# Expert stage of a two-layer kernel: the ids are turned ahead of the similarities on TensorE and ScalarE, and GpSimd gates the rows of `up` ahead of the slots' ids

## The reference, cut to what matters

```python
h = layernorm(x) * (1 + cb) + sb
q = batch_normalised(h @ w_q)                   # per token 2 sides x 8 heads x 128
sim = einsum('pbnhd,hkpd->pbnhk', q, keys)      # 32 keys on each side
sx, ix = top_k(sim[0], 8)
sy, iy = top_k(sim[1], 8)
scores, pk = top_k(sx[..., :, None] + sy[..., None, :], 8)   # 8 of 64 pairs
indices = (ix * 32 + iy) taken at pk            # ids of 8 experts per head
w = softmax(scores) * gelu(h . down_embed[indices])
x = x + gb * sum of w * up_embed[indices]
```

## Time and profile before

| | |
|---|---|
| runs of the kernel before, us | 3028.55 median of 3 (3027.59 to 3028.96) |
| the profiled execution, us | 3042.62, with a span of 3040.8 |
| busy, of the span | TensorE 91%, VectorE 75%, ScalarE 72%, GpSimd 58% |
| 29 units of the expert stage, from 1944.42 to 2759.18 us | 814.76 |
| of them busy | VectorE 771.62, TensorE 739.68, ScalarE 520.69, GpSimd 276.86 |
| mean granted TensorE clock there | 0.78 of full speed |

### The profile page before, as it was taken

The page is one execution under the profiler, slowest core; times in us unless marked ns, Lnnn a source line. Parts: engine busy times, 40 slices in busy tenths (PEclk is TensorE's granted clock), DMA queues, the critical chain, the costliest instruction groups (busy, mean ns, idle before and its releaser), DMA issues. The chain is left out here.

```text
span 3040.8 us, 77592 instructions
## 1 busy us (share of the span) xinstructions
PE 2775.4 (91%) x27940; PEld 2091.0 (69%) x27940; DVE 2294.6 (75%) x8471; ACT 2180.4 (72%) x4273; POOL 1777.8 (58%) x1756
## 2 busy tenths in 40 slices
PE   5999999999999999999999985799989899998688
PEld 3777777777777777777777774566666666666443
DVE  5676776767767767767767645899999999997565
ACT  3888888887888887887887860566666666665575
POOL 3788887788779878878778770333333333331111
PEclk7999999999999999999999996687777777777799
DMA  3000000000000000000000003000000000000000
GB/s 103 1 1 8 1 1 8 1 1 8 1 1 8 1 1 8 1 1 8 1 1 8 1 8 123 1 0 0 0 0 0 0 0 0 0 0 2 8 21 28
DMA packets 11793, 27.63 MB, mean 9 GB/s; under 512 B 1529, under 2 KB 6137, under 8 KB 11137
## 3 DMA queue, kind: packets, MB, share of 16 engines
q1 hardware_dynamic: 11618, 25.48, 2.5%
HBM read 17.07 MB, written 8.40 MB: 8 GB/s over the span
## 5 line engine op out<-in xcount | busy, mean ns | idle before, releaser
L284 POOL TENSOR_TENSOR probs_l<-probs,probs_h 128x512 fp32r<-128x512 f32 x1024 | 1302.3, 1294 | 342.7 <-ACT probs_h L378 339.0
L377 ACT ACTIVATE probs<-bank 128x512 f32<-128x512 f32 x1024 | 636.0, 621 | 280.3 <-PE bank L698 200.7
L539 DVE TENSOR_REDUCE maxes<-ring 128x1 f32<-128x512 f32 x1024 | 659.7, 686 | 185.0 <-PE ring L678 184.2
L378 ACT ACTIVATE probs_h<-bank 128x512 fp32r<-128x512 f32 x1024 | 636.9, 622 | 0.0
L697 PE MATMUL bank<-q_hh,k_hl 128*128 128x512 f32 x1024 | 425.7, 416 | 1.8 <-ACT probs_h L378 1.6
L698 PE MATMUL bank<-q_lm,k_h 65*128 65x512 f32 x1024 | 406.7, 397 | 0.0
L708 PE MATMUL obank<-probs_h,x_l 128*128 128x512 f32 x1024 | 405.5, 396 | 0.0
L710 PE MATMUL obank<-probs_h,x_h 128*128 128x512 f32 x1024 | 404.5, 395 | 0.0
L709 PE MATMUL obank<-probs_l,x_h 128*128 128x512 f32 x1024 | 403.8, 394 | 0.0
L678 PE MATMUL ring<-k_hl,q_hh 128*128 128x512 f32 x1024 | 339.3, 412 | 12.0 <-DVE maxes L539 7.4
L1074 ACT ACTIVATE low_hot<-obank 128x512 f16<-128x512 f32 x512 | 296.9, 603 | 66.0 <-PE obank L1249 52.9
(11 more groups left out here) (252 smaller groups left out, 4986.2 us busy)
## 6 DMA issues: line engine op xcount, KB each, us to landing
xt<-in_x SPq DMA_DIRECT2D x8, 512.0 KB, 9.5
out_x<-xt SPq DMA_DIRECT2D x8, 512.0 KB, 2.6
x<-out_x SPq DMA_DIRECT2D x1, 4096.0 KB, 12.1
out_x<-x SPq DMA_DIRECT2D x16, 256.0 KB, 2.1
mod<-out_x SPq DMA_DIRECT2D x3, 512.0 KB, 13.7
pk_wq<-in_w_q SPq DMA_DIRECT2D x1, 1024.0 KB, 5.9
pk_wqT<-in_w_qT SPq DMA_DIRECT2D x1, 1024.0 KB, 7.4
hot_rule<-in_hot_rule SPq DMA_DIRECT2D x1, 776.0 KB
```

Of the source, the lines that this page charges most:

```text
L284: nc.gpsimd.tensor_tensor(probs_l[:, i, :], probs[:, s % 4, :], probs_h[:, i, :].bitcast(F32), ALU.subtract).then_inc(low_ready, 1)
L377: nc.scalar.activation(probs[:, s % 4, :], st[s % 4], ACT.Exp)
L378: nc.scalar.activation(probs_h[:, i, :], st[s % 4], ACT.Exp).then_inc(st_free[s % 4], 1)
L539: nc.vector.tensor_reduce(maxes[:, i, k:k + 1], ring[bank_of(at)][:], AX.X, ALU.max).then_inc(rows_maxed, 1)
```

## The change

Three lists of calls are put in another order; no instruction is added or removed.

```diff
@@ ScalarE's loop @@
                 exponentials(u + 1)
                 centred(u + 2)
-                sims_out(u + 2, 0)
                 split_ids(u + 1)
                 turned_ids(u + 1)
+                sims_out(u + 2, 0)
                 sims_out(u + 2, 1)
                 middle(u + 1, True)
@@ TensorE's loop @@
                 turn_h(u + 2)
+                turn(u + 1)
                 similarities(u + 2, 0)
-                turn(u + 1)
                 similarities(u + 2, 1)
                 activations(u + 1)
@@ GpSimd's loop @@
                     candidates(u + 1)
-                    slots(u + 1)
                     if i == 3:
                         pool.wait_ge(out_full, 4 * b + 4)
                         gate_up(b + 1)
+                    slots(u + 1)
                     stage(u + 2)
```

## The result

| | before | changed |
|---|---|---|
| runs, us | 3029.89 median of 6 (3027.59 to 3040.68) | 3003.72 median of 6 (2996.10 to 3013.54) |
| ratio | 1 | 0.9913, 95% interval 0.9888 to 0.9937 |
| the profiled execution, us | 3042.62, span 3040.8 | 2996.10, span 2994.3 |

The change is faster by 0.9%, 26 us from median to median; forecast were 24. The two profiled executions differ by more, 46.5 us. Of that, 18.9 us lie ahead of the first `low_hot` (1911.34 against 1892.47), in the attention, which the change doesn't touch: the changed kernel's profile is the fastest of its six runs, and the one of the kernel before took longer than any of its six. It repeats well: 790.87 us here and 791.01 in a later execution of the same kernel.

A forecast was written before the change was run, and what follows sets the result against it. The slots chain was taken to bound the expert-stage unit: 26.93 + 0.9 - 0.5 = 27.3 us against 28.10. Over 29 units 23 us, with the first unit 24, from 3028.55 to 3004 us; range 2986 to 3014.

The forecast's parts named there:

- The wait that goes: VectorE's `low_hot` wait for the ids, 33.7 us in 22 units, goes whole; turn 0.6 us behind the split.
- The chain that takes its place: Turn, two similarities, activations, weights, slots, L1153, split, next turn: 26.93 us before two corrections, 27.3 after, setting the period.
- The collision: The six slot additions on GpSimd meet VectorE's L1149 and L1150: 0.9 us more a unit, bounds 0.54 and 1.16.
- The clock: TensorE's clock rises to 2.4 GHz 4.6 us behind the turn, making similarities and first activations 0.5 us shorter.
- (a): VectorE's own chain of work in a unit, with `low_hot` directly behind `weigh`: 26.73 us.
- VectorE is the bound: Rival: slots stay clear of L1149, so VectorE's own 26.73 us a unit holds; 2988 us in all, chance 0.26.
- `gate_up`: GpSimd multiplication in 7 of 29 units, moved ahead of the slots: unit stays 27.3 us, at highest 27.8 with L1142 held.
- the exclusive lock: Skill's rule that two-SBUF-input VectorE and GpSimd instructions exclude each other: L1142 held, sum 3.5 us higher, about 3009 us.
- The first unit: The loop's first unit, 33.08 us, loses the wait ahead of the turn: about 1 us, bounds 0 and 2.
- The last: The last two units, like attention and layer 1, are not changed: 0.
- Slower: Rival: idleness ahead of the turn keeps the clock's rise late, with full collision; 28.87 us a unit, 3051 us, chance 0.04.

The follow-up runs named there:

- the run with the ids' numbers early: Against the changed kernel, ScalarE makes the next unit's found-index numbers ahead of its last two `low_hot` copies; 29 units 765.56 us, again 765.03, against 790.87.
- the tables behind the slots: Against the changed kernel, VectorE waits for the slots before L1149 and L1150 and not behind them; 29 units 790.83 us against 790.87.
- the filler: Against the changed kernel, four unneeded 96x512 matmuls on TensorE between `turn_h` and the turn of the ids; 29 units 775.78 us, 15.1 less.

## Why the prediction was right, and where it was not

- **The wait that goes.** As the first part said: cast 0.11 us behind the split, turn 0.58 us behind it (0.6 expected), the wait of `low_hot` gone, TensorE idle for 1.83 us ahead of the turn, which delays nothing in the turn itself. The two totals of 33.7 us in the earlier trace rows are equal by chance and are not the same time: VectorE waits 22 times, up to 4.6 us, TensorE 29 times, up to 1.7. And the 4.6 belongs to the loop's first unit, so that VectorE's waits inside the 29 were 29.1 us.
- **The chain that takes its place.** Right as a mechanism: L1153 waits for L1364 in all 29 units, and the run with the ids' numbers early shows that this chain and not VectorE bounds the unit. By the rows of the profile, in a unit from turn to turn (2273.76 to 2301.08), the chain is 0.70 + 4.26 + 1.45 + 10.48 + 3.96 + 2.23 + 0.12 + 3.52 + 0.59 = 27.31 us.
- **The collision** was priced 0.9 us and took 0.70 (2.23 - 1.53); that VectorE's instructions cause it is shown by the tables behind the slots.
- **The clock** was priced 0.5 us less for a rise 4.6 us behind the turn. It rises at 4.95, and the gain was 0.15 (1.45 for 1.60 behind the activations' start). In the kernel before, the latest rise was at 5.87 and not 5.77. And it is no term of a sum: it gives way to the other terms. That 26.93 + 0.9 - 0.5 came out at 27.3 was in part luck: the mechanism that holds the unit there is one the prediction didn't have, and the errors of the two corrections, with 0.18 us less from L1153 to the split, cancel.
- **VectorE's own time**, (a), was too high: 26.73 against 26.3. The 0.16 us of the earlier trace rows is given back by the next instruction, since MAX8 starts 6.95 us behind `low_hot` in both kernels. And the 3.70 us from L1153 to the split held a meeting with GpSimd's `hc_stage` copy (L1169 took 0.56 us beside it, and 0.33 elsewhere); now this stretch takes 3.52. These two make 0.34 of the 0.43 us; the rest is open. The rival "VectorE is the bound" was therefore priced 12 us too slow. It describes not this kernel, but those that beat it.
- **`gate_up`** was charged nothing against the other units, and that held: 27.30 with and without. That L1142 is held was seen as the upper bound, 1.1 us; it cost 0.33 us, hidden in the slack ahead of L1153, where such a unit waits 0.44 us and not 0.65. So the 3.5 us more of the sum by the exclusive lock didn't come (that sum should have read 3008 us, not 3009). What I missed is that the long units before were in part the clock's.
- **The first unit** was put at 1 us, bounds 0 and 2, and lost 4.1. There TensorE is late, not the split: from the end of its turn of the tokens to the turn of the ids took 4.04 us and takes 0.77, so the whole similarity and its eviction are saved, and not only a wait. Another 1.0 us is in its first activations, at a mean granted clock of 0.79 and not 0.73. **The last** took 0.9 us more, put at 0. In the two profiles the expert stage thus gained 27.1 us (23.9 + 4.1 - 0.9), against 24 forecast and 26 between the medians: here too errors of opposite sign.
- **Slower** by a late rise didn't happen. The idle time ahead of the turn does cost clock, as the filler shows, some half a microsecond a unit (15.1 us in 29).

## What to carry to other kernels

When a wait is removed by moving work behind a critical instruction, write down the longest chain that starts there in the new order, and ask whether moving one engine's list alone would do: here ScalarE's order gave the gain (with `gate_up`'s place 47.7 us of the 29 units), and TensorE's took half of it back (23.9 are left). A GpSimd instruction on a chain wants a place where VectorE runs nothing with two SBUF inputs. And where the granted clock changes in every pass, a small saving or a small cost on the chain may not show at all; test with something larger, or with a delay.

## What was not expected of the hardware

- A loop can lock to the changes of TensorE's clock. Three different lists of work (the change, a copy of 0.30 us more, the tables moved) all ran at 27.31 us a unit, with the rise at 4.95, 4.28 and 4.25 us behind the turn.
- Four matmuls that nobody needs, where TensorE would stand idle, made 29 units 15.1 us shorter, in one execution.
- VectorE's L1142 (f32, two SBUF inputs) is held by a GpSimd multiplication, 0.62 us for 0.29, while the 16 MAX8 of L1140, beside the same multiplication, take 1.38 us as elsewhere.
